# State-space layer with a magnitude branch: the order of the eight output jobs that close phase 0

## The reference

```python
xn = _layernorm(x, axis=-1)                       # x: 16384 tokens x 1024
delta = softplus(einsum('btd,ed->bte', xn, Wd) + bd)
a_pos = softplus(a_log) + 0.0001                  # 1024 x 16 states
def step(state, inp):                             # over the tokens
    a_bar = exp(-dt * a_pos)
    state = a_bar * state + dt * b_param * x_t
    return (state, state.sum(-1))
attn = einsum('btd,ed->bte', y, Wo) + bo
real = einsum('bti,io->bto', xn, cos(theta + theta_noise))
imag = einsum('bti,io->bto', xn, sin(phi + phi_noise))
out = x + attn + sqrt(real * real + imag * imag)
```

## Time and profile before

| | |
|---|---|
| median of 2 runs | 1100.62 us (1099.55 to 1101.69) |
| the profiled execution | 1100.78 us, of it 1098.8 us span on core 1 |
| spans of the eight cores | 1089.9 to 1098.8 us |
| VectorE busy | 818.1 us, 74% of the span |
| TensorE matmul / ScalarE / GpSimd busy | 52% / 53% / 14% |
| granted TensorE clock, mean of core 1 | 0.695 |
| last scan of phase 0 to first scan of phase 1 | 309.3 to 408.56 us |

### The profile page before, as it was taken

One profiled execution on the slowest core, in us unless ns is written; L12 is line 12 of the kernel. 1 busy time (PEld: TensorE's weight loads), 2 busy tenths in 40 slices (PEclk: granted clock), 3 DMA queues, 4 the chain that ended last, 5 costly groups with the idle time before them and its releaser, 6 DMA issues.

```text
span 1098.8 us, 9306 instructions; the slowest of 8 cores (1089.9 to 1098.8 us)
## 1 busy us (share of the span) xinstructions
PE 569.3 (52%) x2248; PEld 239.1 (22%) x2248; DVE 818.1 (74%) x721; ACT 582.1 (53%) x924; POOL 159.1 (14%) x127
## 2 busy tenths in 40 slices
PE   1333344445467464565545447656555554454785
PEld 1211011111123230122212114333222211121343
DVE  5279888989843449999999992434899999999423
ACT  5784766776623245566665542322466655565330
POOL 2478000000012100000000001120000000000232
PEclk9965555656669875666666568886766655666799
DMA  8777101100013300000000002231100000000023
GB/s 247 213 204 210 56 25 30 29 20 1 0 48 95 101 23 1 0 1 0 1 0 1 0 1 56 88 123 44 44 1 0 0 1 1 1 0 1 30 72 114
DMA packets 36323, 51.65 MB, mean 47 GB/s; under 512 B 3120, under 2 KB 19760, under 8 KB 36272
## 3 DMA queue, kind: packets, MB, share of 16 engines
q1 hardware_dynamic: 33584, 42.68, 13.8%
q0 software_dynamic: 2688, 8.39, 2.3%
HBM read 42.67 MB, written 8.39 MB: 46 GB/s over the span
## 4 chain that ended last, share of the span: by engine, by line
DVE 42%; PE 20%; issue 17%; ACT 16%; DMA 2%; DVEq 1%; SPq 0%; POOL 0%; ACTq 0%; POOLq 0%
DVE grot L760 36%; ACT abar L714 9%; PE pd L883 6%; PE pt L607 3%; PE pt L617 3%; PE pd L296 2%; DVE sfm L897 2%; ACT bdg_bf L177 2%; DMA xsub<-xin 2%; PE pe L377 1%; PE py L911 1%; DMA sfm<-xin 1%; DVE xsub L439 1%; PE pt L377 1%; PE py L377 1%
## 5 line engine op out<-in xcount | busy, mean ns | idle before, releaser
L760 DVE TENSOR_TENSOR_SCAN grot<-abar,gcar,vbuf 128x768 bf16<-128x768 f32 (+1 forms) x384 | 660.0, 1780 | 39.0 <-ACT abar L714 31.3
L714 ACT ACTIVATE abar<-delta,nega 128x768 f32<-128x768 f32 (+1 forms) x384 | 340.4, 896 | 246.3 <-DVE grot L760 243.0
L798 PE MATMUL pe<-grot,bdg_bf 128*128 128x384 bf16 x256 | 86.3, 441 | 121.4 <-DVE grot L760 121.3
L798 PE MATMUL py<-grot,bdg_bf 128*128 128x384 bf16 x256 | 86.2, 444 | 120.0 <-DVE grot L760 120.0
L296 PE MATMUL pd<-xnbf,wd_bf 128*128 128x384 bf16 (+1 forms) x368 | 95.4, 438 | 20.7 <-ACT xsub L315 14.7
L785 PE MATMUL py<-grot,bdg_bf 128*128 128x512 bf16 x64 | 33.7, 538 | 78.6 <-DVE grot L760 78.6
L657 POOL TENSOR_TENSOR xsub<-r,i 128x384 f32<-128x384 f32 (+1 forms) x9 | 18.1, 2011 | 382.6 <-ACT i L649 382.6
L883 PE MATMUL pd<-ybf,wo_bf 128*128 128x384 bf16 (+1 forms) x320 | 70.8, 370 | 0.0
L607 PE MATMUL pt<-xnbf,cos_bf 128*128 128x384 bf16 (+1 forms) x320 | 70.5, 369 | 0.0
L785 PE MATMUL pe<-grot,bdg_bf 128*128 128x512 bf16 x64 | 33.9, 540 | 70.0 <-DVE grot L760 69.9
L617 PE MATMUL pt<-xnbf,sin_bf 128*128 128x384 bf16 (+1 forms) x320 | 64.5, 346 | 0.0
(11 more groups left out here) (107 smaller groups left out, 560.1 us busy)
## 6 DMA issues: line engine op xcount, KB each, us to landing
xsub<-xin SPq DMA_DIRECT2D x14, 512.0 KB, 4.3
xres<-xin SPq DMA_DIRECT2D x32, 192.0 KB, 2.4
out<-osub POOLq DMA_DIRECT2D x32, 192.0 KB, 2.6
xres<-xin SPq DMA_DIRECT2D x8, 256.0 KB, 3.8
out<-osub POOLq DMA_DIRECT2D x8, 256.0 KB, 3.2
etmp<-tht SPq DMA_DIRECT2D x6, 256.0 KB, 4.7
r<-thn SPq DMA_DIRECT2D x6, 256.0 KB, 5.8
r<-pht SPq DMA_DIRECT2D x6, 256.0 KB, 3.3
```

What stands on the lines that cost most here:

```text
L714: sx = run("scalar", lambda e, sl=sl_ab, par=par, dt=dt, n=n, tp=tp: e.activation(out=abar[:, sl * TP:sl * TP + tp], in_=delta[:, par * TP ...
L760: vs = run("vector", lambda e, g=gsl, sl=sl_ab, par=par, dt=dt, n=n, tp=tp: e.tensor_tensor_scan(out=grot[:, g * TP:g * TP + tp], data0=ab ...
L798: td = run("tensor", lambda e, c=c, g=gsl, dt=dt, n=n, bb=ypair[c]: e.matmul(bb[:, 0:384], bdg_bf[:, (dt * NST + n) * P:(dt * NST + n + 1) ...
```

## The change

Only the loop over the output jobs of phase 0 changes, and the ring slots of its magnitudes 5, 6 and 7.

- The matmuls and the chains of magnitudes 2 to 7 are emitted two by two in iterations 0, 1 and 2, ahead of the subtile and of the output job. Before, one was emitted in each of iterations 0 to 5, its chain behind the subtile.
- Subtiles of phase 1 in the loop: 0 in iteration 1; 5 and then 1 in iteration 3; 2 in iteration 4; 3 in 5; 4 in 6. None is left for after the loop.
- After iteration 6 the first softplus and the first product of phase 1 are done ahead, with the `pt` banks, as phase 1 already does for phase 2. They are emitted ahead of output job 7.
- Magnitudes 5, 6 and 7 move from ring slots 5, 8, 6 to 7, 10, 11, which do not lie on the halves of `delta` and `vbuf` that the work done ahead writes.
- Phases 1 and 2 keep their order (`ffn_d2` gives the same jobs in the same iterations).

```diff
             def rslot(i):
+                if p == 0 and i in (5, 6, 7):
+                    return {5: 7, 6: 10, 7: 11}[i]
                 m = {5: 5, 6: 8, 7: 6, 8: 7, 9: 9}
...
             if p == 0:
-                a_sched = {1: [0], 3: [5], 6: [1], 7: [2, 3]}
+                a_sched = {1: [0], 3: [5, 1], 4: [2], 5: [3], 6: [4]}
+                ffn_d2 = {0: [2, 3], 1: [4, 5], 2: [6, 7]}
             else:
                 a_sched = {1: [0], 3: [1], 4: [2],
                            9: [3], 10: [4], 11: [5]}
+                ffn_d2 = {i: [NFC + i] for i in range(nch - NFC)}
             for it in range(nch):
                 dt, c0, wdth = cjobs[it]
-                if NFC + it < nch:
-                    emit_ffn_mm(NFC + it)
+                for jb in ffn_d2.get(it, []):
+                    emit_ffn_mm(jb)
+                    if p == 0:
+                        emit_ffn_chain(jb)
...
-                if NFC + it < nch:
-                    emit_ffn_chain(NFC + it)
+                if p != 0:
+                    for jb in ffn_d2.get(it, []):
+                        emit_ffn_chain(jb)
...
-                if p == 1 and it == 12:
+                if (p == 0 and it == 6) or (p == 1 and it == 12):
                     a_xnbf_s[p + 1] = a_last[0]
                     a_x32_v[p + 1] = a_last[1]
                     emit_sp_mm(p + 1, 0, pt, [("pt", 0), ("pt", 1)])
```

## The result

The changed kernel takes 1113.31 us (median of 7 runs, 1112.76 to 1115.53), the kernel before 1102.67 us (6 runs, 1099.55 to 1104.86). The ratio is 1.0101, 95% interval 1.0086 to 1.0117: slower by 1%, inside the 2% that I called no change, and 1.3 us above my range (1102 to 1112, forecast 1107.5). The same two programs, run later on another occasion, gave 1111.91 us against 1104.91 us, ratio 1.0061 (1.0032 to 1.0089). In some executions the cores of one die show a lower granted clock and the time is some per cent longer; the medians and run counts here include such executions, the ratios and their intervals do not.

The account below looks back on a forecast made before the run. The prediction took a chain of handovers between phase 0's last scan and phase 1's first as the bound, with no engine full. Its terms summed to +6.9 us on 1100.78, giving 1107.7; forecast 1107.5, range 1102 to 1112.

Parts of the forecast that it names:

- the stretch: From the last scan of phase 0 to the first of phase 1: 99.2 us before, predicted to grow by 6.9.
- Iterations 0 and 2: Packed magnitude blocks stand ahead of the Wo block on TensorE: +3.46 us in the first, +3.48 in the second.
- the part behind R6: From the residual add of iteration 6 to phase 1's first scan: 7.13 us instead of 31.91, −24.78.
- Iteration 1: Subtile 0's Ln waits behind two magnitude chains in ScalarE's queue: 19.45 us instead of 13.19, +6.26.
- Iteration 3: Subtile 1's load must wait for subtile 5's transposes, same half of `xsub`: 23.9 us instead of 13.55, +10.35.
- Iterations 4 and 5: Each takes in a subtile already loaded: two times 10.90 us instead of 13.69 for both, +8.11.
- Iteration 6: Takes subtile 4 instead of subtile 1: 10.90 us as before, 0.
- Rival 1: Packed matmuls keep TensorE's clock at its upper level: up to 10.3 us saved, 1097 us, chance 0.07.
- Rival 3: Four loads going out together at about 361 cost more: 1110 to 1113 us, chance 0.13.
- Rival 4: Job 7 runs during the softplus done ahead: at most 3.9 us less, 1103.6; counted in another rival's 0.12.

Follow-up runs that it names:

- e7_sub_first: The changed kernel with subtile 0 ahead of magnitudes 4 and 5 (matmuls and chains) in iteration 1: 1113.2 us (one run).
- e3_parity: The changed kernel with subtile order 0; 5 and 2; 1; 4; 3, no two in a row sharing a half of `xsub`: 1109.32 us, ratio 1.0036.
- e4_warm: The changed kernel with matmuls of no use ahead of the subtiles' transposes, where TensorE idles: 1103.87 us, ratio 0.9990 against the kernel before.
- e6_before_warm: The kernel before with matmuls of no use ahead of its subtiles' transposes in the loop: 1095.64 us, ratio 0.9916.
- e2_ahead: The kernel before with its own magnitude order, subtiles 1 to 4 all in iteration 6, new ring slots and work done ahead: 1099.78 us, ratio 0.9959.

## Why the prediction was wrong, and where it was right

**The base was the step that failed first.** The sum starts from the profiled execution's 1100.78 us and the median of two runs, 1100.62. The kernel before took 1102.67 (6 runs, those two among them) when it was run beside the changed one, and on later occasions 1104.86 (26 runs), 1104.91 (16), 1104.22 (10) and 1103.12 (7): the two runs were at its low end. Of the 5.8 us by which I missed 1113.31, 2.1 are this by the first occasion and 4.3 by the later ones. My range took in bounds for each unknown cost, but nothing for a base from two runs.

**The second is the size of the change, since I took one core for eight.** I had +6.9; the stretch grew by 8.4. The views showed core 1, one of the two slowest. In its rows iterations 1 and 3 cost 13.19 and 13.55; over all cores they are 12.3 and 12.3, on the quickest 10.7 and 10.9, because there the transposes and the Wo block behind the load were still at the upper clock. That is 2.1 us too much on the side of before. On core 1 itself, in the first pair of profiles, the stretch grew by 6.65 (99.22 to 105.87), which is my sum; from the slowest core of the one to the slowest of the other (core 5, 107.58) it grew by 8.36, as over all cores.

The whole time grew by 10.6 us on the first occasion and by 7.0 on the second, the stretch by 8.3 in either pair of profiles. What made the 2.2 more on the first occasion stays open.

**The terms.** Iterations 0 and 2 and the part behind R6 were right within 0.15. *Iteration 1*: +7.0 for +6.3, and the reason I gave is in the trace. I wrote that the Ln stands behind two chains in ScalarE's queue and runs at 332.75, with the transposes at 334.73; they are at 333.12 and 335.08. What the prediction did not ask is what this wait could be exchanged for: e7_sub_first removes it by giving up the cover of the four blocks, and loses. *Iteration 3*: +10.6 for +10.35, of it 3.7 is the exposed load, shown by e3_parity. *Iterations 4 and 5*: 10.6 each instead of 10.90, +7.5 for +8.11. *Iteration 6*: +1.1 for 0. Two rows show it in the changed kernel:

```profile
402.06 0.81 DVE L439 TENSOR_SCALAR xsub<-xsub,rstd,negmr 128x1024 f32<-128x1024 f32 x1 [0.46 <-DVE negmr L435]
```

```profile
404.76 3.62 PE L890 MATMUL pd<-ybf,wo_bf 128*128 128x512 bf16 x8
```

The Wo block is at half the clock throughout (3.62, in the earlier trace rows 3.01), and the normalizing starts 0.35 us later than in any other subtile; it does so in both profiles, and e4_warm's 9.3 beside 9.0 has the same 0.35. I did not find what holds it.

**The rivals.** Rival 1 (the clock rises by the packing) went the other way: the transposes took 1.08 or 1.09 at every subtile of the core shown, and the clock is part of the loss, as e4_warm and e6_before_warm show. The row that I counted for it, transposes at 325.35 in 0.63 after 3.64 us of idle, has another right behind it in the kernel before that I did not read:

```profile
326.26 3.57 PE L883 MATMUL pd<-ybf,wo_bf 128*128 128x512 bf16 x8
```

The clock had fallen there too, one block later. And the idle alone does not tell when: on core 0 the same transposes took 1.09 after 3.09 us of idle. The advice of the Trainium skill that stood beside it (TensorE: Matmul & The Clock Gate, "HAM oscillation — how this bites in real kernels") is about doing matmuls together ahead of a wait; here the packed blocks ran at the upper clock (1.73 start to start), and the transposes behind the waits that followed, of 4.57 to 8.58 us, ran at half of it (1.08 and 1.09). Rival 3 (more loss by the loads) did not happen: subtile 5 was read 2.5 us behind R2 in the mean (3.0 on core 5) and subtile 1 10.0 later, as summed. Rival 4 did not happen: R6 to the first scan took 7.19 for 7.13. What I said the range leaves out is 0.20 by my own chances (0.07 + 0.06 + 0.065), not 0.17.

## What to carry to other kernels

The matmuls that lay beside a wait for a load or a norm were free here; packed together in iterations 0 and 2 they cost their length, 3.5 us each time, and the waits left behind ran their own matmuls at half the clock. A wait on an in-order queue is worth what its removal gives, less what the new order uncovers: in iteration 1 an order without it brought the transposes 5.7 us earlier and uncovered 6.9 us of matmuls. Form differences over all cores rather than from the slowest one, and widen the range by the spread of the base where that is two runs. To free a load, move what lies in its buffer: a table of slots and one schedule line took 8.7 us off e2_ahead, and 14 off the kernel before.

## What the runs showed of the hardware that I had not expected

In one profiled execution of the kernel before (before_again), TensorE ran on cores 0 and 1 at a rate that is neither of the two I had seen. First core 1, then core 3, the same blocks:

```profile
334.32 2.27 PE L607 MATMUL pt<-xnbf,cos_bf 128*128 128x512 bf16 x8
336.42 2.27 PE L617 MATMUL pt<-xnbf,sin_bf 128*128 128x512 bf16 x8
```

```profile
332.93 1.89 PE L607 MATMUL pt<-xnbf,cos_bf 128*128 128x512 bf16 x8
334.65 1.89 PE L617 MATMUL pt<-xnbf,sin_bf 128*128 128x512 bf16 x8
```

Start to start a block takes 2.10 us on core 1 and 1.72 on core 3, and the windows give a granted clock of 0.77 and 0.93 over the same 40 us (330 to 370). It cost these two cores 6 and 7 us: stretches of 103.9 and 105.0 beside 95.9 to 101.4, mean 97.9, on the others. The Trainium skill (TensorE: Matmul & The Clock Gate, "Seeing it yourself") tells of a limiter that takes a whole die to 13/16 of the clock when three of its cores run dense matmuls; 1.72 × 16 / 13 is 2.12, which agrees with the 2.10, but cores 2 and 3 of the same die kept the full rate in that stretch, which does not agree with "the whole die". Later in the same execution it was the other pair. In the last output jobs, 1060 to 1080, the windows of core 0 and then of core 3 are:

```profile
1060.00:1080.00 20.00, 16.15 (x99) 9.37 (x97) 4.71 (x8) 7.50 (x15) 6.39 (x8) 1.00 0.22 69
1060.00:1080.00 20.00, 17.25 (x89) 9.50 (x88) 3.53 (x6) 6.58 (x13) 5.48 (x7) 0.81 0.22 68
```

Core 1 has 1.00 there and core 2 0.81, which is 13/16. So in this execution the slow rate was with two cores of the die at a time, and not always the same two. What sets it off, no run here shows.
